# Two pairs of score tiles at a time on TensorE: one burst of products, then a projection piece behind each of the next two scores

## The chip, the cores and the metric

The kernel runs on one core of one Trainium2 chip. The metric is the time of the whole program on the device in microseconds (us), and all times here are in that unit unless another one is named. The engines are TensorE (PE, with PEld for its weight loads), VectorE (DVE), ScalarE (ACT), GpSimd (POOL) and SyncE (SP, which issues most DMAs).

## The reference

Input is x of 8 batches, 1024 tokens, 512 channels, with 16 heads of 32 channels. A block has two halves, each with a shift, a scale and a gate from a small modulation. The first half is an attention, the second a feed-forward network on the 512 tokens of each batch that a router picks. The loop of the change computes the first half:

```python
q = (x @ Wq + bq).reshape(b, h, dh, t)
k = (x @ Wk + bk).reshape(b, h, dh, t)
v = (x @ Wv + bv).reshape(b, h, dh, t)
attn = jnp.einsum('bhdt,bhds->bhts', k, v) * temperature
attn = jax.nn.softmax(attn, axis=-1)
out = jnp.einsum('bhdt,bhts->bhds', q, attn)
...
x = x + ga * _L0_attn_ref(h, ...)
```

The scores are k times v, the softmax runs over s, and the result is q times the probabilities. The reshape cuts the flat (token, channel) rows, so a head takes 64 successive tokens.

## The kernel before

The attention half runs over 8 batches of 4 groups. A group holds 4 heads (256 tokens) and 32 score tiles of 128 by 1024, called units. Two units are a pair (`p` from 0 to 15, `h2` 0 or 1), and a group has 16 pairs in two halves of 8. Seven batches run in a loop on every engine (`Fori`), the last one is written out behind it, and each engine has its own instruction stream in a fixed order; semaphores join them.

For each unit TensorE makes the score tile with two matmuls of 512 columns (`scores_of`, L551 to L560) in one of three slots of PSUM (`slot`, L361). VectorE takes the negated row maximum (`row_max`, L971 to L976). ScalarE takes the exponential with that as its bias, and sums the rows (`exp_unit`, L809 to L817); it then frees the slot (`slot_free`) for the unit three further on. The probabilities lie in eight buffers, that is four pairs. For every second pair VectorE divides q by the row sums (`q_over_sums`, L1026 to L1039, two instructions: `rinv` and `qn`). TensorE multiplies `qn` with the probabilities (`products`, L598 to L607: eight instructions of 32 output rows each), four pairs behind the scores (`LAG`), into the bank `acc`; eight pairs are summed there. VectorE then evacuates `acc` with the gate (`gated`, L1008 to L1013, after the first maximum of pairs 3 and 11), and that frees the bank for the first products of pairs 4 and 12 (`acc_free`, L680).

Beside that, TensorE computes k, v and q of the next group in sixteen pieces into one PSUM bank `pj`: four slices of k and v with three pieces of four matmuls each (`kv_slice`, L562 to L571), two slices of q with two pieces of twelve half-wide matmuls each (`q_slice`, L573 to L584). ScalarE evacuates them (`evac_kv`, after the first exponential of pairs 2, 5, 8 and 11, L850; `evac_q`, after that of pairs 13 and 15), and GpSimd adds the bias and splits them in two halves of float16 (`split_kv`, L1289 to L1298). SyncE copies the halves into the stacks that the scores of the next group read (`replicate`, L427 to L434). After pair 9 TensorE also transposes the normalised x of the group after the next into a score slot (`transposes`, L586 to L592, called at L714 to L717), and ScalarE evacuates that in four instructions (`evac_t`).

TensorE's order in a pair is: first score, the products of four pairs earlier, second score, one piece of a projection (L673 to L713). In the very last group there are no projections; there four transposes of kept tokens stand behind pairs 6, 9, 12 and 14 (L684 to L691).

VectorE's other work of a group sits between the maxima, in the order of L1104 to L1131: `qn` behind the second maximum of each even pair, the gating behind the first maximum of pairs 3 and 11, the dot product with the router behind pairs 1 and 15, statistics of x2 (the residual sum) behind pairs 5 and 7 and of the next x behind pairs 9 and 13. In the last batch it also ranks the scores of the first batch (`rank_first`, L1074).

GpSimd's work of a group hangs on `qn`: `behind_qn(b, g, j)` (L1353 to L1356) waits for the division behind pair 2j. Behind 2 it adds the residual (x2), behind 6 it splits the transposed x and multiplies h with the gate row for `base` (`base_times`, L1343), and behind 7 it adds x2 to `base` (`base_plus`, L1348), after which SyncE stores the rows (`store_rows`, L506).

Of the kernel before, what the change touches and what calls it, by code (L numbers as in the profile page):

```python
# [16 lines left out]
PAIRS = SUBS * (T // P)  # L17
GB = T // TG
NG = B * GB
# [107 lines left out]
def block_phases(nc, x, w_qkv, b_qkv, temperature, w_router, w_ffn, c, w_mod, out, h_rows, mod_rows, sel_rows, score_rows, r):  # L127
# [16 lines left out]
    with ExitStack() as ctx:  # L144
# [94 lines left out]
        aux = [pj[:], acc[:]]  # L239
# [14 lines left out]
        ft_lo = sem("ft_lo")  # L254
# [50 lines left out]
        s_ht = sem("s_ht")  # L305
# [35 lines left out]
        T_AT = 20  # L341
# [203 lines left out]
        def stk_count(b, g):  # L545

            return b * (128 * GB // 2) + 128 * (g // 2 + 1)

        @block.tensor
        def _(pe):  # L550
            def scores_of(b, g, p, h2):  # L551

                v = ring_at(p, h2)
                hq, i = 2 * (p // NQ) + h2, p % NQ
                pe.wait_ge(slot_free, freed(b, g, v))
                for half in range(2):
                    mm = nc.tensor.matmul(slot(g, v)[:, half * D:(half + 1) * D],  # L557
                                          stacks[g % 2][:, 0, hq, i * P:(i + 1) * P],
                                          stacks[g % 2][:, 1, hq, half * D:(half + 1) * D], start=True, stop=True)
                mm.then_inc(score_pe, 1)  # L560

            def kv_slice(par, kk):  # L562

                w, p = (wk16, wv16)[kk // 2], kk % 2
                terms = [(cc, a, z) for cc in range(CC) for a, z in ((0, 0), (1, 0), (0, 1))]
                for t, (cc, a, z) in enumerate(terms):
                    mm = nc.tensor.matmul(pj[:], hT16[par][:, a, cc, p * P:(p + 1) * P], w[:, z, cc, :],  # L567
                                          start=(t == 0), stop=(t == len(terms) - 1))
                    if t in (3, 7):
                        yield  # L570
                mm.then_inc(kv_pe, 1)  # L571
# [22 lines left out]
            def whole(piece):  # L594
                for _ in piece:
                    pass

            def products(p):  # L598

                i = p % NQ  # L600
                for h2 in range(2):
                    for half in range(2):
                        at = DH * (2 * h2 + half)
                        mm = nc.tensor.matmul(acc[at:at + DH, :], qn[:, (p // 2) % 2, p % 2, h2, :],  # L604
                                              probs[:, (2 * p + h2) % PROBS, half * D:(half + 1) * D],
                                              start=(i == 0), stop=(i == NQ - 1))
                return mm  # L607
# [51 lines left out]
            def transpose_kept(n, cc, dst):  # L659

                if cc == 0:
                    pe.wait_ge(s_gh[n % 2], 16 * KT * (n // 2 + 1))
                for kt in range(KT):
                    mm = nc.tensor.transpose(dst[:, kt * P:(kt + 1) * P], hs[n % 2][:, kt, cc * P:(cc + 1) * P], ident[:])
                mm.then_inc(ft_pe, 1)

            def body(b, last):
                for g in range(GB):
                    n4 = b * (GB * 4) + 4 * (g + 1)
                    n2 = b * (GB * 2) + 2 * (g + 1)  # L670
                    nxt = (g + 1) % 2
                    end = last and g == GB - 1
                    for p in range(PAIRS):  # L673
                        if p % NQ == 0:
                            for k in range(2):
                                pe.wait_ge(s_stk[k][g % 2][p // NQ], stk_count(b, g))

                        scores_of(b, g, p, 0)
                        pe.wait_ge(qn_done, b * (GB * PAIRS // 2) + g * (PAIRS // 2) + p // 2 + 1)
                        if p in (LAG, LAG + NQ):  # L680
                            pe.wait_ge(acc_free, b * (GB * SUBS) + g * SUBS + (p - LAG) // NQ + 2)
                        products((p - LAG) % PAIRS).then_inc(pv_done, 1)
                        scores_of(b, g, p, 1)
                        if end:  # L684
                            if p in KEPT_AT:
                                cc = KEPT_AT.index(p)
                                if cc == 0:
                                    pe.wait_ge(q_evac, 2 * NG)
                                else:
                                    pe.wait_ge(ft_lo, cc)  # L690
                                transpose_kept(0, cc, aux[0])  # L691
                        elif p < 12:
                            if p % 3 == 0:
                                if p == 0:
                                    pe.wait_ge(s_ht, b * GB + g + 2)
                                    pe.wait_ge(q_evac, n2)
                                else:
                                    pe.wait_ge(kv_evac, n4 + p // 3)
                                piece = kv_slice(nxt, p // 3)
                                next(piece)  # L700
                            elif p % 3 == 1:
                                next(piece)
                            else:
                                whole(piece)
                        elif p % 2 == 0:
                            if p == 12:
                                pe.wait_ge(kv_evac, n4 + 4)
                            else:
                                pe.wait_ge(q_evac, n2 + 1)
                            piece = q_slice(nxt, (p - 12) // 2)  # L710
                            next(piece)
                        else:
                            whole(piece)  # L713
                        if 2 * p + 2 == T_AT and not (last and g >= GB - 2):  # L714
                            pe.wait_ge(s_xhat, b * GB + g + 3)
                            pe.wait_ge(slot_free, freed(b, g, T_AT))
                            transposes(slot(g, T_AT))  # L717
# [522 lines left out]
        def _(pool):  # L1240
# [102 lines left out]
            def base_times(b, g):  # L1343

                par = (g + 1) % 2
                times_row(base[:, par], hbuf[:, par], 3, ALU.mult, b * (3 * GB) + 3 * g + 3)
# [6 lines left out]
            def behind_qn(b, g, j):  # L1353


                wait_alone(qn_done, b * (GB * PAIRS // 2) + g * (PAIRS // 2) + j + 2)  # L1356
# [16 lines left out]
            def body(b, last):  # L1373
                for g in range(GB):
                    n4 = b * (GB * 4) + 4 * (g + 1)
                    n3 = b * GB + g + 3
                    nxt = (g + 1) % GB
                    prep = not (last and g >= GB - 2)
                    end = last and g == GB - 1

                    behind_qn(b, g, 0)
                    if prep:
                        pool.wait_ge(t_pe, b * GB + g + 2)
                        normed_x((g + 2) % 4, n3)
                    behind_qn(b, g, 1)
                    if end:
                        gather_h(0, h_rows[0:T])
                    else:
                        split_kv(nxt, 0, n4 + 1)
                    behind_qn(b, g, 2)  # L1390
                    residual(b, g)
                    behind_qn(b, g, 3)
                    if not end:
                        split_kv(nxt, 1, n4 + 2)
                    normed_before(b, g)
                    if last and g == GB - 2:
                        wait_alone(r.s_slot, 1)
                        store_kept(nc, r, sel_rows, range(0, TB // 4))
                    behind_qn(b, g, 4)
                    if not end:  # L1400
                        split_kv(nxt, 2, n4 + 3)
                    h_times(b, g)
                    behind_qn(b, g, 5)
                    h_plus(b, g)
                    if not end:
                        split_kv(nxt, 3, n4 + 4)
                    behind_qn(b, g, 6)
                    if prep:
                        split_hT(g % 2, n3, (slot_free, freed(b, g, T_AT) + SLOTS))
                    base_times(b, g)  # L1410
                    if last and g == GB - 2:
                        store_kept(nc, r, sel_rows, range(TB // 4, TB // 2))
                    behind_qn(b, g, 7)
                    base_plus(b, g)
                    if last and g == GB - 2:
                        store_kept(nc, r, sel_rows, range(TB // 2, TB))
# [69 lines left out]
```

## Time and profile before

| | us |
|---|---|
| three runs, median (lowest to highest) | 2372.16 (2371.15 to 2373.54) |
| the profiled execution, its own time | 2367.9 |
| its span, from the first to the last instruction | 2366.2 |
| PE busy in the span | 2271.7 (96%) |
| DVE busy in the span | 1918.0 (81%) |
| ACT busy in the span | 1484.9 (63%) |
| POOL busy in the span | 1240.9 (52%) |
| granted TensorE clock, mean | 0.991 of full speed |

The attention half fills the first two thirds of the span and the feed-forward half the rest. Busy times count an instruction from its start to its end, and successive instructions of an engine overlap a little, so the distance from one start to the next is what an instruction costs a busy engine. In a timeline row the columns are the start, the duration, the engine, line and operation, the names and shapes, the number of merged instructions, and in brackets the idle time before the first and what ended it.

### The profile page before, as it was taken

The page shows a single profiled execution, that of the slowest core. Times are in us where ns is not written, and L with a number is a line of the kernel's source. Part 1 is how long each engine was busy: PE and PEld are TensorE (multiplying, and loading weights), DVE is VectorE, ACT ScalarE, POOL GpSimd, SP SyncE. Part 2 cuts the span into 40 slices and gives each one's busy share as a digit, 9 for nine tenths or more (in the row PEclk, how much of TensorE's full clock was granted, in tenths as well). Part 3 has the DMA queues.
Part 4 walks back from the last instruction along what each step waited for, and adds up shares of the span by engine and source line. Part 5 has one row for each costly group of instructions (what it writes and reads, how often), then busy time and mean ns, then how long its engine had stood idle before and what let it go on. Part 6 is the DMA issues. An engine that isn't in the chain of part 4 may idle for free.

```text
span 2366.2 us, 40899 instructions
## 1 busy us (share of the span) xinstructions
PE 2271.7 (96%) x12772; PEld 879.5 (37%) x12772; DVE 1918.0 (81%) x2908; ACT 1484.9 (63%) x2616; POOL 1240.9 (52%) x1117
## 2 busy tenths in 40 slices
PE   7999999999999999999999999887979999999998
PEld 2333333333333333333333333231434444444443
DVE  5899999999999999999999999998844654654543
ACT  1788888888888888888888888777411111111111
POOL 4666676667766667666766676554523212212300
PEclk9999999999999999999999999998989999999999
DMA  7232333333333333323334333224422021111100
GB/s 218 69 95 72 82 87 84 81 86 80 73 92 82 76 84 88 88 70 92 75 80 101 73 74 83 67 55 116 134 67 68 18 67 50 39 47 50 58 19 18
DMA packets 123765, 180.76 MB, mean 76 GB/s; under 512 B 44112, under 2 KB 44112, under 8 KB 123480
## 3 DMA queue, kind: packets, MB, share of 16 engines
q1 hardware_dynamic: 113760, 152.30, 25.9%
q0 software_dynamic: 9728, 25.23, 3.5%
q8 instruction: 117, 1.92, 0.3%
q14 instruction: 160, 1.31, 0.2%
HBM read 67.17 MB, written 43.16 MB: 47 GB/s over the span
## 4 chain that ended last, share of the span: by engine, by line
PE 57%; DVE 21%; issue 10%; POOL 5%; ACT 3%; DMA 1%; SPq 1%; DVEq 0%; POOLq 0%; ACTq 0%
DVE nmax L975 15%; PE sc L738 13%; PE sc L751 13%; PE sc L557 10%; PE acc L604 10%; PE pj L579 6%; PE pj L567 4%; POOL x L1318 3%; ACT probs L815 2%; DVE stats L1018 1%; DVE qn L1036 1%; DVE x L1013 1%; ACT room L788 1%; DVE rinv L1031 1%; POOL sel_rows L123 1%
## 5 line engine op out<-in xcount | busy, mean ns | idle before, releaser
L815 ACT ACTIVATE probs<-sc,nmax 128x1024 f32<-128x1024 f32 x1024 | 1136.7, 1116 | 240.4 <-DVE nmax L975 235.4
L975 DVE TENSOR_REDUCE nmax<-sc 128x1 f32<-128x1024 f32 x1024 | 1217.7, 1213 | 56.3 <-PE sc L557 50.0
L604 PE MATMUL acc<-probs,qn 128*32 128x512 f32 x4136 | 552.7, 607 | 9.3 <-DVE x L1013 6.7
L567 PE MATMUL pj<-room 128*128 128x512 f16 x1536 | 393.1, 379 | 0.4 <-ACT qT L805 0.4
L893 ACT ACTIVATE probs<-sc,b_col 128x512 f32<-128x512 f32 x128 | 88.0, 687 | 469.6 <-PE sc L738 440.3
L751 PE MATMUL sc<-room,probs 128*128 128x512 f16 x1536 | 352.1, 379 | 0.0
L557 PE MATMUL sc<-stacks 128*128 128x512 f16 x1024 | 309.4, 384 | 20.1 <-ACT probs L815 18.2
L557 PE MATMUL sc<-room 128*128 128x512 f16 x1024 | 307.7, 382 | 19.2 <-ACT probs L815 7.3
L1197 DVE CAST probs<-probs 128x512 f16<-128x512 f32 x128 | 58.1, 454 | 255.1 <-ACT probs L893 209.7
L751 PEld LDWEIGHTS sc<-room,probs 128*128 128x128 f16 x1536 | 150.3, 98 | 181.3
L567 PEld LDWEIGHTS pj<-room 128*128 128x128 f16 x1536 | 147.6, 98 | 187.9 <-ACT room L788 11.3
L815 ACT ACTIVATION_READ_ACCUMULATOR probs<-sc,nmax 128x1 f32 x1024 | 205.9, 201 | 0.0
L579 PE MATMUL pj<-room 128*128 128x256 f16 x1536 | 188.3, 273 | 1.1 <-ACT qT L805 0.9
L1294 POOL TENSOR_TENSOR room<-room,k_bias 128x512 f32<-128x512 f32 x64 | 81.4, 1272 | 197.7 <-DVE qn L1036 115.9
L557 PEld LDWEIGHTS sc<-stacks 128*128 128x128 f16 x1024 | 75.5, 98 | 291.3 <-ACT probs L815 185.4
L557 PEld LDWEIGHTS sc<-room 128*128 128x128 f16 x1024 | 75.7, 97 | 287.6 <-ACT probs L815 165.5
L738 PE MATMUL sc<-stacks,room 128*128 128x512 f16 x768 | 176.2, 379 | 0.0
L604 PEld LDWEIGHTS acc<-probs,qn 128*32 128x32 f32 x4136 | 81.9, 108 | 230.6 <-issue 227.0
L579 PEld LDWEIGHTS pj<-room 128*128 128x128 f16 x1536 | 150.0, 98 | 45.8 <-ACT qT L805 2.3
L1327 POOL TENSOR_TENSOR hbuf<-hbuf,rows 128x1024 f32<-128x1024 f32 x66 | 155.5, 2356 | 17.0 <-DVE qn L1036 16.7
L738 PE MATMUL sc<-qT,room 128*128 128x512 f16 x512 | 163.3, 381 | 0.1
L1298 POOL TENSOR_TENSOR room<-room 128x512 f16<-128x512 f32 x128 | 148.9, 1163 | 10.7
(146 smaller groups left out, 2241.1 us busy)
## 6 DMA issues: line engine op xcount, KB each, us to landing
room<-room SPq DMA_DIRECT2D x512, 64.0 KB, 2.0
stacks<-room SPq DMA_DIRECT2D x512, 64.0 KB, 2.0
h_rows<-hbuf SPq DMA_DIRECT2D x132, 128.0 KB, 2.3
out<-base SPq DMA_DIRECT2D x132, 128.0 KB, 2.4
room<-in_L_attn_x SPq DMA_DIRECT2D x96, 128.0 KB, 2.6
rows<-mod_rows SPq DMA_DIRECT2D x32, 256.0 KB, 3.8
room<-in_L_ffn_W SPq DMA_DIRECT2D x8, 1024.0 KB, 5.1
probs<-in_L_wmod SPq DMA_DIRECT2D x4, 1024.0 KB, 7.8
```

The lines of the kernel that those rows point to most:

```text
L557: mm = nc.tensor.matmul(slot(g, v)[:, half * D:(half + 1) * D], stacks[g % 2][:, 0, hq, i * P:(i + 1) * P], stacks[g % 2][:, 1, hq, half * ...
L567: mm = nc.tensor.matmul(pj[:], hT16[par][:, a, cc, p * P:(p + 1) * P], w[:, z, cc, :], start=(t == 0), stop=(t == len(terms) - 1))
L579: mm = nc.tensor.matmul(pj[:, ci * 2 * P:(ci + 1) * 2 * P], wq16[:, z, cc, co * P:(co + 1) * P], hT16[par][:, a, cc, :], start=(t == 0), s ...
L604: mm = nc.tensor.matmul(acc[at:at + DH, :], qn[:, (p // 2) % 2, p % 2, h2, :], probs[:, (2 * p + h2) % PROBS, half * D:(half + 1) * D], st ...
L738: mm = nc.tensor.matmul(ff[f % 2], w1_16[:, z, cc, f * P:(f + 1) * P], fT16[n % 2][a][:, cc, :], start=(t == 0), stop=(t == len(terms) - 1))
L751: mm = nc.tensor.matmul(ff2[kt], g16[:, nth(n, FC, f) % 3, a, kt * P:(kt + 1) * P], w2_16[:, z, f, :], start=(f == 0 and t == 0), stop=(f ...
L815: nc.scalar.activation(probs[:, u % PROBS, :], slot(g, ring_at(p, h2)), ACT.Exp, bias=nmax[:, u % PROBS:u % PROBS + 1], accum_out=rsum[:, ...
L893: nc.scalar.activation(g32[:, f % 2, :], ff[f % 2], ACT.Gelu_apprx_tanh, bias=b1_col[:, f:f + 1], scale=1.0 / WS).then_inc(gelu_done, 1)
L975: nc.vector.tensor_reduce(nmax[:, u % PROBS:u % PROBS + 1], slot(g, ring_at(p, h2)), AX.X, ALU.max, negate=True).then_inc(max_done, 1)
L1294: nc.gpsimd.tensor_tensor(kv32[kk % 2][:], kv32[kk % 2][:], row, ALU.add).then_inc(kv_bias, 1)
L1298: nc.gpsimd.tensor_tensor(dst[:, 1], kv32[kk % 2][:], dst[:, 0], ALU.subtract).then_inc(kv_split, 1)
L1327: nc.gpsimd.tensor_tensor(dst, a, rows[:, row:row + 1, :].broadcast_to([P, SUBS, D]), op).then_inc(s_hm, 1)
```

## The change

TensorE's loop goes in steps of two pairs. A step is: first score of the even pair, the products of both earlier pairs in one burst, second score of the even pair, a piece, first score of the odd pair, a piece, second score of the odd pair. In the steps of pairs 2 and 8 the last two are exchanged. The pieces come from one generator for the whole group, with the same waits and in the same order; the transposes stand behind the step of pair 8. On GpSimd `base_times` moves from the end of the work behind the sixth `qn` to behind the seventh.

```diff
+            def projections(b, g):
...
+                for kk in range(4):
+                    if kk == 0:
+                        pe.wait_ge(s_ht, b * GB + g + 2)
+                        pe.wait_ge(q_evac, n2)
+                    else:
+                        pe.wait_ge(kv_evac, n4 + kk)
+                    yield from kv_slice(nxt, kk)
+                    yield
+                for s in range(2):
+                    if s == 0:
+                        pe.wait_ge(kv_evac, n4 + 4)
+                    else:
+                        pe.wait_ge(q_evac, n2 + 1)
+                    yield from q_slice(nxt, s)
+                    yield
+            def first_transposes():
+                for p in range(PAIRS):
+                    if p in KEPT_AT:
...
+                        transpose_kept(0, cc, aux[0])
+                    yield
...
-                    for p in range(PAIRS):
+                    pieces = first_transposes() if last and g == GB - 1 else projections(b, g)
+                    for p in range(0, PAIRS, 2):
...
                         scores_of(b, g, p, 0)
                         pe.wait_ge(qn_done, b * (GB * PAIRS // 2) + g * (PAIRS // 2) + p // 2 + 1)
                         if p in (LAG, LAG + NQ):
                             pe.wait_ge(acc_free, b * (GB * SUBS) + g * SUBS + (p - LAG) // NQ + 2)
                         products((p - LAG) % PAIRS).then_inc(pv_done, 1)
+                        products((p + 1 - LAG) % PAIRS).then_inc(pv_done, 1)
                         scores_of(b, g, p, 1)
...
+                        next(pieces)
+                        scores_of(b, g, p + 1, 0)
+                        if p in (2, 8):
+                            scores_of(b, g, p + 1, 1)
+                            next(pieces)
                         else:
-                            whole(piece)
-                        if 2 * p + 2 == T_AT and not (last and g >= GB - 2):
+                            next(pieces)
+                            scores_of(b, g, p + 1, 1)
+                        if 2 * p + 4 == T_AT and not (last and g >= GB - 2):
                             pe.wait_ge(s_xhat, b * GB + g + 3)
                             pe.wait_ge(slot_free, freed(b, g, T_AT))
                             transposes(slot(g, T_AT))
...
                     if prep:
                         split_hT(g % 2, n3, (slot_free, freed(b, g, T_AT) + SLOTS))
-                    base_times(b, g)
                     if last and g == GB - 2:
                         store_kept(nc, r, sel_rows, range(TB // 4, TB // 2))
                     behind_qn(b, g, 7)
+                    base_times(b, g)
                     base_plus(b, g)
```

## Rows read from the trace of the kernel before

**Rows 1.** The page, chain that ended last: shares of the span by engine.
```profile
PE 57%; DVE 21%; issue 10%; POOL 5%; ACT 3%; DMA 1%; SPq 1%; DVEq 0%; POOLq 0%; ACTq 0%
```

**Rows 2.** Timeline of TensorE, group 1 of batch 4: scores, products, pieces.
```profile
899.06 0.59 PE L557 MATMUL sc<-stacks 128*128 128x512 f16 x2
...
904.71 0.59 PE L557 MATMUL sc<-stacks 128*128 128x512 f16 x2
905.24 1.07 PE L604 MATMUL acc<-probs,qn 128*32 128x512 f32 x8
906.24 0.60 PE L557 MATMUL sc<-stacks 128*128 128x512 f16 x2
906.68 1.03 PE L567 MATMUL pj<-room 128*128 128x512 f16 x4
907.54 0.59 PE L557 MATMUL sc<-stacks 128*128 128x512 f16 x2
...
936.44 1.47 PE L579 MATMUL pj<-room 128*128 128x256 f16 x12
...
947.58 0.59 PE L557 MATMUL sc<-room 128*128 128x512 f16 x2
```

**Rows 3.** Timeline of all engines around the transposes of that group.
```profile
926.32 1.11 ACT L815 ACTIVATE probs<-sc,nmax 128x1024 f32<-128x1024 f32 x1
...
927.58 1.09 PE L590 MATMUL sc<-ident,room 128*128 128x128 f32 x8
...
928.72 0.61 PE L557 MATMUL sc<-stacks 128*128 128x512 f16 x2
...
929.37 1.23 DVE L975 TENSOR_REDUCE nmax<-sc 128x1 f32<-128x1024 f32 x1 [0.28 <-PE sc L557]
```

**Rows 4.** Timeline of all engines, that group: VectorE's rows of k0 to k3.
```profile
905.19 0.85 DVE L1004 SCALAR_TENSOR_TENSOR dot_out<-hbuf,router_row 128x512 bf16<-128x512 f32 x1
...
905.98 2.34 DVE L975 TENSOR_REDUCE nmax<-sc 128x1 f32<-128x1024 f32 x2
...
908.24 0.16 DVE L1031 RECIPROCAL rinv<-rsum 128x4 f32<-128x4 f32 x1
...
908.65 1.22 DVE L975 TENSOR_REDUCE nmax<-sc 128x1 f32<-128x1024 f32 x1
...
909.78 0.68 DVE L1013 TENSOR_TENSOR x<-acc,rows 128x512 f32<-128x512 f32 x1
...
910.38 3.47 DVE L975 TENSOR_REDUCE nmax<-sc 128x1 f32<-128x1024 f32 x3
...
913.77 0.17 DVE L1031 RECIPROCAL rinv<-rsum 128x4 f32<-128x4 f32 x1
...
916.90 0.69 DVE L1018 BATCH_NORM_STATS2 stats<-x 128x6 f32<-128x512 f32 x1 [0.31 <-POOL x L1318]
...
922.44 0.68 DVE L1018 BATCH_NORM_STATS2 stats<-x 128x6 f32<-128x512 f32 x1
...
923.43 2.32 DVE L975 TENSOR_REDUCE nmax<-sc 128x1 f32<-128x1024 f32 x2
```

**Rows 5.** Timeline of all engines, that group: ScalarE's rows of k1.
```profile
907.30 1.11 ACT L815 ACTIVATE probs<-sc,nmax 128x1024 f32<-128x1024 f32 x1 [0.79 <-DVE nmax L975]
...
908.41 0.68 ACT L788 ACTIVATE room<-pj,tempw_col 128x512 f32<-128x512 f32 x1
...
908.98 1.11 ACT L815 ACTIVATE probs<-sc,nmax 128x1024 f32<-128x1024 f32 x1
...
911.63 1.11 ACT L815 ACTIVATE probs<-sc,nmax 128x1024 f32<-128x1024 f32 x1 [0.35 <-DVE nmax L975]
```

**Rows 6.** Timeline of TensorE at the end of attention: products of two pairs.
```profile
1658.57 1.92 PE L604 MATMUL acc<-probs,qn 128*32 128x512 f32 x16
```

**Rows 7.** Timelines of GpSimd and of SyncE's queue at that group's end.
```profile
945.37 2.37 POOL L1351 TENSOR_TENSOR base<-base,x 128x1024 f32<-128x1024 f32 x1 [0.33 <-DVE qn L1036]
...
938.99 10.02 SPq L433 DMA_DIRECT2D room<-room  x16
```

## What I predict, and from what

> **What bounds the kernel now.** I read the page's chain first [rows 1]: TensorE holds 57% of it and VectorE 21%, so in the attention loop two engines take turns. Then I read the timeline of one steady group (group 1 of batch 4) engine by engine; a "cycle" is two pairs, four score tiles a, b, c, d, and k0 to k7 are the eight cycles of a group.
>
> TensorE [rows 2]: from a pair's first score to its products 0.53, products to second score 1.00, second score to the piece 0.44, piece 0.86. That is 2.83 a pair, 5.66 a cycle. A piece of q products is 1.47 long against 1.03, so it takes 0.45 more: 1.31, and such a cycle (k6, k7) 6.55. The transposes of k4 take 1.14 [rows 3]. Six times 5.66, twice 6.55 and 1.14 are 48.20; the group took 48.52 (899.06 to 947.58) [rows 2]. So TensorE waited 0.32 in a whole group, and it looks like the bound.
>
> VectorE [rows 4]: two maxima take 2.26 (905.98 to 908.24), so one takes **1.13**; reciprocal and qn 0.41; the gating between c and d 0.60 (909.78 to 910.38); the dot of k0 0.79; the statistics about 0.61, with the aggregate of k3 0.99. From 905.98 to 923.43, three cycles, it paused only for x2 (0.31 before 916.90): 5.82 a cycle, more than TensorE's 5.66. TensorE's first scores stood at 904.71 and, three cycles later, at 921.69; VectorE took them up 1.27 and 1.74 later. **VectorE already sets the pace in k1 to k4**, and the three score slots let TensorE hide it until the transposes.
>
> The ring [rows 3, 5]: a score tile's maximum can start 0.65 after its first matmul (928.72 to 929.37), its exponential 1.25 after the maximum began (910.38 to 911.63; I use 1.26), and the score that takes over the slot 1.26 after the exponential began (926.32 to 927.58). So a slot turns round in at least 3.17, plus whatever VectorE or ScalarE is late.
>
> **The change part by part.**
>
> *The burst.* Products of two pairs follow each other. At the end of attention the trace has such a burst, 16 matmuls of 1.92 [rows 6], 0.85 more than the 1.07 of eight [rows 2]; 1.00 + 0.85, rounded up to 1.86, against twice 1.00. One switch from score to products becomes score to piece, 0.44 for 0.53. A cycle of TensorE is then 0.53 + 1.86 + 0.44 + 0.86 + 0.44 + 0.86 + 0.44 = **5.43** (before 5.66), with q pieces **6.33** (before 6.55). Unheld, a group is 6 x 5.43 + 2 x 6.33 + 1.14 = 46.38, which is 1.82 under 48.20. In k1 and k4 the order c, d, piece has the same sum. The Trainium skill ("TensorE: Matmul & The Clock Gate", Part 3) says that a weight load overlaps running matmuls only where the row groups differ; products use all 128 rows, so by it the second pair would cost its full 1.00 and the burst 2.00. The row at the end of attention gives 1.86; the other value is a rival below.
>
> *The slot of b.* The next a uses the slot of b. Before, b started 1.53 behind a, and the next a 4.13 behind b. Now b starts 2.39 behind a, and the next a is due 3.04 behind b, less than the 3.17 of an idle ring. So even with every other engine ready a cycle is 5.56, and each tenth by which VectorE or ScalarE is late holds TensorE up. VectorE is late: that is the step on which I decide.
>
> *The walk.* I carry the three engines through a group by the rows above, times from its first score, with VectorE 2.00 behind at a. F is when b's slot is free (its maximum plus 2.52, or later where ScalarE is held); "due" is TensorE unheld.
>
> | k | a | max a | max b | F | due | next a | held |
> |---|---|---|---|---|---|---|---|
> | 0 | 0 | 2.00 | 3.13 | 5.65 | 5.43 | 5.65 | 0.22 |
> | 1 | 5.65 | 7.72 | 8.85 | 11.90 | 11.08 | 11.90 | 0.82 |
> | 2 | 11.90 | 13.25 | 14.93 | 17.45 | 17.33 | 17.45 | 0.12 |
> | 3 | 17.45 | 19.80 | 20.93 | 23.45 | 22.88 | 23.45 | 0.57 |
> | 4 | 23.45 | 25.72 | 26.85 | 29.90 | 28.88 | 31.04 | 1.02 |
> | 5 | 31.04 | 31.69 | 34.07 | 36.59 | 36.47 | 36.59 | 0.12 |
> | 6 | 36.59 | 38.56 | 40.06 | 42.58 | 42.92 | 43.36 | 0.44 |
> | 7 | 43.36 | 45.29 | 46.42 | 48.94 | 49.69 | 49.69 | 0 |
>
> Line k1 in full. VectorE ends k0 at 2.00 + 4 x 1.13 + 0.41 + 0.79 = 7.72 and does a, then b at 8.85. ScalarE starts a's exponential at 8.98, needs 1.11 for it (907.30 to 908.41) and then, before b's, does the evacuation of a projection, 0.57 (908.41 to 908.98) [rows 5]: 8.98 + 1.11 + 0.57 + 1.26 = 11.92, in the table 11.90. TensorE was due at 5.65 + 5.43 = 11.08. In the other lines: k2, b is ready only at 14.29 + 0.65, so VectorE idles 0.55, and the statistics wait for x2 as now (3.13 behind the reciprocal at 913.77) [rows 4]; k4, the same evacuation, and the transposes take b's slot, so the 1.02 falls before them; k5, VectorE has caught up at a and waits 1.25 for b behind the burst; k6, the burst waits for the gating (begins at 36.83, 0.68 long, plus 0.05) where it was due at 37.12. That wait is old, but the products now stand 2.27 behind the start of c instead of 3.36; behind it are queued the burst, b, c and d, and VectorE's b. k7 ends with VectorE 1.94 behind, so the walk closes on itself.
>
> The holds add up to 3.31 and the gain was 1.82: a group of **49.69 against 48.52, 1.17 more**. VectorE's account agrees: from b of k0 to b of k4 it needs 23.72, before 4 x 5.82 or some 23.3; the gains of the q cycles are less than what it idles at b of k2, k5 and k6.
>
> *What costs nothing.* The odd pair's products move ahead of a score and a piece; they need the same qn as the even pair's, so no wait is new there, and the exponential of a waits for products that end 1.6 behind a's start, before its maximum ends. The kept-token transposes keep their piece numbers. GpSimd's multiplication for base moves behind the next qn: with the addition (2.37, ending 0.16 into the next group now) [rows 7] it ends some 3 into the next group, before GpSimd's next call at the qn of k0 (4.7). SyncE's stores then wait for it; now they wait until 949.01, 1.43 into the group, for the copies of the stacks, so they come up to 2 later, and SyncE has nothing else urgent until x2 of k2. Were that cover gone, the price would be those 2 once a group, 56 in all; the other end is a gain of the little that it hinders qn of k7, under 0.4, in a cycle where VectorE is not what ends last. I take 0. The second stack copies start behind the last projection split; eight of the sixteen (half of 10.02) [rows 7] are needed by the next group, and the walk leaves them about half a microsecond.
>
> **The sum.** 28 groups in the seven looped batches by 1.17 are 33. The last batch's first three groups have ranking work on VectorE; between 0 and 1.17 each, I take 0.5 each, 1.5 in all, because a longer VectorE cycle gives the slots more time. The last group has no projections: 0. Together +34 on the profiled execution's 2367.9, which gives 2402. The median of the runs is 4.3 above that execution, so **2406**. About 0.2% is what a measurement of this kernel can tell from no change.
>
> **Rivals.**
> 1. *The slots only just hold* (faster). If VectorE is never behind at b, a cycle is 5.56 and a group 6 x 5.56 + 2 x 6.33 + 1.14 with the old 0.32 of waits, 47.48: 1.04 x 28 or 29 less, **2343**. For it: TensorE's near-full timeline, with little waiting. Against it: the growing lag of 1.27 to 1.74. It decides at b: where VectorE takes b up at once and no evacuation lies between, F meets the due time to about a tenth.
> 2. *VectorE keeps its pace everywhere*: it is late but never idles at b of k2, k5 and k6, so only the q cycles gain, 0.14 and 0.25 a group: 11 less, **2361**. Against it: a's lead is used up at the transposes.
> 3. *Holds and gains cancel*, with the lag a few tenths smaller: **2372**.
> 4. *The burst is no cheaper than its parts*, 2.00, the change not doing what it says: 0.14 a cycle, passed on in about five cycles of eight, 0.7 x 28 or 20 more than forecast: **2426**. Against it stands the burst of rows 6, so its chance is small.
>
> **How the numbers follow.** Forecast 0.67 (its own range 2390 to 2425: holds 0.4 a group either way, and the last batch), rival 1 0.08, rival 2 0.12, no change 0.07, rival 4 0.06. Faster 0.20, same 0.07, slower 0.73. The range 2355 to 2428 takes in the forecast, rivals 2, 3 and 4, and leaves rival 1 out.
>
> **What would show it.** Right: bursts of 16 at 1.86; groups of 49.7; TensorE idle some 3.3 a group before a, named for the exponentials, most in k1 and k4; VectorE idle over a microsecond for b in k5. Wrong: groups of 47.5 with hardly a wait at a (rival 1), or VectorE without pauses (rival 2); then the walk's lag at a is the step that failed.

## The result, and the profile after

| | before | after |
|---|---|---|
| median of four runs each (lowest to highest) | 2372.60 (2371.15 to 2373.54) | 2474.57 (2470.43 to 2476.25) |
| span of the profiled execution | 2366.2 | 2474.5 |

The ratio is 1.0428, 95% interval 1.041 to 1.0446: the changed kernel is 102 us slower. The forecast was 2406 with a range up to 2428, so the sign was right and the size was not.

The page of after: busy time of the engines, shares of the chain that ended last [rows 1], and two of the costliest groups (count | busy, mean ns of one | idle before them, and what ended most of it).

```profile
PE 2273.3 (92%) x12772; PEld 909.4 (37%) x12772; DVE 1956.1 (79%) x2908; ACT 1490.1 (60%) x2616; POOL 1243.8 (50%) x1117
...
PE 52%; DVE 23%; issue 13%; ACT 5%; POOL 4%; DMA 1%; SPq 1%; DVEq 1%; ACTq 0%; POOLq 0%
...
L986 DVE TENSOR_REDUCE nmax<-sc 128x1 f32<-128x1024 f32 x1024 | 1215.5, 1214 | 121.1 <-PE sc L557 116.3
L604 PE MATMUL acc<-probs,qn 128*32 128x512 f32 x4136 | 516.8, 619 | 25.9 <-DVE x L1024 21.3
```

TensorE is as busy as before (2271.7), in a longer span. Two lines say where to look. VectorE's maxima sat idle for 121.1 waiting for scores (56.3 before), which the walk foresaw. And VectorE's busy time grew from 1918.0 to 1956.1, by 38, though it has the same 2908 instructions: something on it became longer, and the prediction has no step for that.

TensorE's timeline of one group of after (start, duration, form, and in brackets the idle time before), from the first score behind the loop's jump to the first score of the next group:

```profile
901.72 0.60 PE L557 MATMUL sc<-room 128*128 128x512 f16 x2 [2.00 <-issue]
...
913.44 0.61 PE L557 MATMUL sc<-room 128*128 128x512 f16 x2
...
925.04 0.60 PE L557 MATMUL sc<-room 128*128 128x512 f16 x2 [0.46 <-ACT probs L826]
...
932.58 0.61 PE L557 MATMUL sc<-room 128*128 128x512 f16 x2
933.11 1.92 PE L604 MATMUL acc<-probs,qn 128*32 128x512 f32 x16
934.97 0.60 PE L557 MATMUL sc<-room 128*128 128x512 f16 x2
...
939.03 1.92 PE L604 MATMUL acc<-probs,qn 128*32 128x512 f32 x16 [0.30 <-DVE x L1024]
...
951.31 0.60 PE L557 MATMUL sc<-stacks 128*128 128x512 f16 x2
```

These are a of k0, k2, k4 and k5 and of the next k0. From the first they stand at 0, 11.72, 23.32, 30.86 and 49.59; the walk has 0, 11.90, 23.45, 31.04 and 49.69. The burst is 1.86 (933.11 to 934.97), and k6's burst waits for the gating. This group is the walk. The next one is not: it takes 51.48 (to 1002.79), and nearly all of the excess over the walk (1.69 of 1.79) is in its k0, which takes 7.34 where the walk has 5.65. The timeline of all engines of after at that place:

```profile
949.68 2.35 POOL L1338 TENSOR_TENSOR base<-hbuf,rows 128x1024 f32<-128x1024 f32 x1 [2.32 <-DVE qn L1047]
...
951.31 0.60 PE L557 MATMUL sc<-stacks 128*128 128x512 f16 x2
...
952.11 2.37 POOL L1362 TENSOR_TENSOR base<-base,x 128x1024 f32<-128x1024 f32 x1
...
952.47 2.57 DVE L1015 SCALAR_TENSOR_TENSOR dot_out<-hbuf,router_row 128x512 bf16<-128x512 f32 x1
...
954.97 2.34 DVE L986 TENSOR_REDUCE nmax<-sc 128x1 f32<-128x1024 f32 x2
...
957.56 0.60 PE L557 MATMUL sc<-stacks 128*128 128x512 f16 x2 [1.09 <-ACT probs L826]
...
958.65 0.61 PE L557 MATMUL sc<-stacks 128*128 128x512 f16 x2 [0.49 <-ACT probs L826]
```

Before, `base_plus` ended 0.16 into the group [rows 7]; VectorE's timeline of before, which the prediction does not show at that place, has the router dot of pair 15 beginning 0.13 ahead of that end:

```profile
947.61 0.68 DVE L1004 SCALAR_TENSOR_TENSOR dot_out<-hbuf,router_row 128x512 bf16<-128x512 f32 x1
```

Now `base_times` stands in front of it, `base_plus` runs from 952.11 to 954.48, and the dot, which reads `hbuf` and `router_row` beside it, takes 2.57 and ends 0.56 after it. The two maxima behind it start at 954.97, 3.66 behind a (the walk has 2.00), and TensorE then waits 1.09 and 0.49 for slots. Over the whole run the dots by their line (shortest, median and longest in ns; the median was 682 before):

```profile
L1015 DVE SCALAR_TENSOR_TENSOR dot_out<-hbuf,router_row x67: 674/1005/2882, 76.2 to 1827.2; 128x512 bf16<-128x512 f32 x67
```

Theory from here: the burst costs what the walk says, about +34, and the move of `base_times` the rest, because a VectorE instruction with two operands in SBUF stands still while GpSimd works on SBUF. The rival: the burst costs it all and the long dot lies in slack.

### The profile page after: what moved, and what is told of

Read it like the earlier page. It is cut to its first block, busy times and chain, and to the rows that moved or that the text cites. A ratio compares the mean times of both kernels' runs of the same rounds, so it can differ in the third digit from the quotient of the medians.

```text
span 2474.5 us, 40899 instructions
## 1 busy us (share of the span) xinstructions
PE 2273.3 (92%) x12772; PEld 909.4 (37%) x12772; DVE 1956.1 (79%) x2908; ACT 1490.1 (60%) x2616; POOL 1243.8 (50%) x1117
## 3 DMA queue, kind: packets, MB, share of 16 engines
q8 instruction: 117, 1.92, 0.3%
## 4 chain that ended last, share of the span: by engine, by line
PE 52%; DVE 23%; issue 13%; ACT 5%; POOL 4%; DMA 1%; SPq 1%; DVEq 1%; ACTq 0%; POOLq 0%
DVE nmax L986 14%; PE sc L749 12%; PE sc L762 12%; PE acc L604 11%; PE sc L557 7%; PE pj L579 6%; ACT probs L826 3%; POOL x L1329 3%; DVE dot_out L1015 3%; ACT room L799 1%; DVE x L1024 1%; PE pj L567 1%; DVE stats L1029 1%; DVE qn L1047 1%; DVE rinv L1042 1%
## 5 line engine op out<-in xcount | busy, mean ns | idle before, releaser
L986 DVE TENSOR_REDUCE nmax<-sc 128x1 f32<-128x1024 f32 x1024 | 1215.5, 1214 | 121.1 <-PE sc L557 116.3
L604 PE MATMUL acc<-probs,qn 128*32 128x512 f32 x4136 | 516.8, 619 | 25.9 <-DVE x L1024 21.3
L557 PE MATMUL sc<-stacks 128*128 128x512 f16 x1024 | 304.3, 384 | 68.9 <-ACT probs L826 67.2
L604 PEld LDWEIGHTS acc<-probs,qn 128*32 128x32 f32 x4136 | 111.2, 111 | 303.3 <-issue 275.1
```

Of the source, the lines that this page charges most:

```text
L986: nc.vector.tensor_reduce(nmax[:, u % PROBS:u % PROBS + 1], slot(g, ring_at(p, h2)), AX.X, ALU.max, negate=True).then_inc(max_done, 1)
```

## The experiments

**1. The burst alone.** After, with `base_times` back in its old place.

```diff
                     behind_qn(b, g, 6)
...
+                    base_times(b, g)
...
                     behind_qn(b, g, 7)
-                    base_times(b, g)
```

> The changed kernel with GpSimd's base_times put back behind the sixth qn; the bursts stay. Theory A (the move costs the missing part): base_plus no longer runs beside the router dot of pair 15, which is 0.68 again instead of 2.57; VectorE is about 2 behind at a of k0 instead of 3.7, and a group takes 49.7 to 50.0 as the walk of the prediction said. Time 2405 to 2425. Rival B (the burst alone accounts for it, and the long dot only fills time that VectorE has to wait anyway): 2465 to 2475, the groups as long as in the changed kernel.

Measured: 2420.27 (2418.99 to 2423.25), ratio 1.0209 [1.0193, 1.0224]. By the distances between the transposes, groups within a batch take 49.79 (before mostly 48.52, the walk 49.69), and the dot is back at a median of 683 ns. Two successive rows of transposes from TensorE's timeline, and the dots by their line:

```profile
908.47 1.10 PE L590 MATMUL sc<-ident,room 128*128 128x128 f32 x8
...
958.25 1.09 PE L590 MATMUL sc<-ident,room 128*128 128x128 f32 x8
```

```profile
L1015 DVE SCALAR_TENSOR_TENSOR dot_out<-hbuf,router_row x67: 673/683/2828, 76.5 to 1776.2; 128x512 bf16<-128x512 f32 x67
```

So the burst costs +50, and the change's other 54 are the move: the theory's place is right.

**2. The move alone.** Before, with `base_times` behind the seventh `qn`.

```diff
-                    base_times(b, g)
...
                     behind_qn(b, g, 7)
+                    base_times(b, g)
```

> The kernel before with only base_times moved behind the seventh qn, no bursts. Theory A: base_times and base_plus run without a pause over the router dot of pair 15, which comes close to the end of base_times. If the dot is held until base_plus ends it takes 2.5 to 3.1 instead of 0.68, VectorE enters k0 some 2 later and never catches up before the transposes: 1.2 to 1.6 a group more, 2405 to 2425. If the dot gets in between the two it takes about 0.9 and the time is 2372 to 2380. Rival B: 2372, no change, whatever the dot takes.

Measured: 2399.34 (2395.38 to 2401.91), ratio 1.0126 [1.011, 1.0141]: between the two theories' numbers. Two of three groups within a batch grow to 50.22 and 50.54, the third stays at 48.56. The timeline of all engines of this kernel in a long and a short one:

```profile
913.64 2.37 POOL L1351 TENSOR_TENSOR base<-base,x 128x1024 f32<-128x1024 f32 x1
...
913.81 2.75 DVE L1004 SCALAR_TENSOR_TENSOR dot_out<-hbuf,router_row 128x512 bf16<-128x512 f32 x1
...
964.04 0.68 DVE L1004 SCALAR_TENSOR_TENSOR dot_out<-hbuf,router_row 128x512 bf16<-128x512 f32 x1
964.17 2.78 POOL L1351 TENSOR_TENSOR base<-base,x 128x1024 f32<-128x1024 f32 x1
```

Where the addition starts first (by 0.17), the dot takes 2.75; where the dot starts first (by 0.13), it takes its 0.68 and the addition 2.78 instead of 2.37. Whoever comes second waits. Which it is hangs on a tenth of a microsecond, and that is why the price is paid in two groups of three. The group across the loop's jump has the long dot too and pays nothing: 49.87 to 50.21, before 49.57 to 50.32. With the bursts every looped group has the long dot, and every group within a batch pays. So the two parts of the change don't add up: 50 and 29 alone, 102 together.

The Trainium skill ("SBUF — State Buffer", section "Who interferes with whom") says that a VectorE instruction with two inputs in SBUF contends with a GpSimd instruction that reads SBUF, for ports that are an exclusive lock, and that "Issue order, not op shape, decides who blocks." Both rows agree, the short dot as well as the long one.

**3. Take away only the overlap.** After, with one wait on GpSimd: `base_plus` starts behind the dot of pair 15.

```diff
                     base_times(b, g)
+                    wait_alone(s_dot, b * (2*GB) + 2*g + 2)
                     base_plus(b, g)
```

> The changed kernel as it is, bursts and move, but base_plus waits for the router dot of pair 15. Nothing else differs, so this is the contention by itself. Theory A: the dot is 0.68 to 0.9, a group 49.6 to 50.0, time 2405 to 2425, like the burst alone; base_plus ends a microsecond later and nobody waits for it. Rival B: 2470 or more, since GpSimd's work only gets later.

Measured: 2425.23 (2419.83 to 2426.85), ratio 1.0224 [1.0207, 1.0241]; the interval overlaps that of experiment 1. Groups of 49.79 again, and the timeline of all engines:

```profile
925.56 2.36 POOL L1338 TENSOR_TENSOR base<-hbuf,rows 128x1024 f32<-128x1024 f32 x1 [2.30 <-DVE qn L1047]
...
928.34 0.68 DVE L1015 SCALAR_TENSOR_TENSOR dot_out<-hbuf,router_row 128x512 bf16<-128x512 f32 x1
...
929.20 2.36 POOL L1362 TENSOR_TENSOR base<-base,x 128x1024 f32<-128x1024 f32 x1 [1.28 <-DVE dot_out L1015]
```

`base_times` is still late, and `base_plus` and the stores behind it are later than in after, yet the 49 us are gone (2474.57 to 2425.23). So it is neither the late stores nor GpSimd's own work; it is the overlap with the dot.

**4. The burst only where a cycle is long.** Before, with the step of two pairs only for p of 12 and 14, where a cycle is 6.33 and the slot of b has time.

```diff
+if p < 12:
+    for q in (p, p + 1):
...
+else:
+    scores_of(b, g, p, 0)
...
+    products((p - LAG) % PAIRS).then_inc(pv_done, 1)
+    products((p + 1 - LAG) % PAIRS).then_inc(pv_done, 1)
+    scores_of(b, g, p, 1)
+    next(pieces)
+    scores_of(b, g, p + 1, 0)
+    next(pieces)
+    scores_of(b, g, p + 1, 1)
```

> Bursts only in the last two cycles of a group (pairs 12 to 15, with the long q pieces), the old order in the other six, base_times at its old place. By the walk (theory A) the slot of b has 3.9 there, so nothing is held and 0.22 is saved twice a group, 0.44 x 28 to 31 or 12 to 14 us: 2358 to 2361. If VectorE sets the pace in these cycles too: 2372, no change. Rival B (a burst costs more than the turn-round of its slot): slower than 2372.

Measured: 2386.80 (2385.01 to 2386.99), ratio 1.0066 [1.0052, 1.008]; groups of 48.95. VectorE's timeline at the end of a group:

```profile
899.50 1.23 DVE L992 TENSOR_REDUCE nmax<-sc 128x1 f32<-128x1024 f32 x1 [0.89 <-PE sc L557]
...
902.99 1.23 DVE L992 TENSOR_REDUCE nmax<-sc 128x1 f32<-128x1024 f32 x1 [0.52 <-PE sc L557]
...
909.29 1.22 DVE L992 TENSOR_REDUCE nmax<-sc 128x1 f32<-128x1024 f32 x1 [0.52 <-PE sc L557]
910.43 0.68 DVE L1021 SCALAR_TENSOR_TENSOR dot_out<-hbuf,router_row 128x512 bf16<-128x512 f32 x1
```

VectorE waits 0.89 for b behind the burst and 0.52 for each fourth score behind its piece: 1.93 in the two cycles. It leaves the group late and pays in the next one, where it sets the pace. The expected 2358 to 2361 counted only TensorE's gain.

**5. The same, with both scores ahead of the burst.** Order for p of 12 and 14: a, b, burst, c, piece, d, piece; TensorE does the same work as in experiment 4.

```diff
 scores_of(b, g, p, 0)
+scores_of(b, g, p, 1)
...
 products((p + 1 - LAG) % PAIRS).then_inc(pv_done, 1)
-scores_of(b, g, p, 1)
-next(pieces)
 scores_of(b, g, p + 1, 0)
 next(pieces)
 scores_of(b, g, p + 1, 1)
+next(pieces)
```

> As the run with bursts only in the last two cycles, but both scores of the even pair stand ahead of the burst and each piece behind a score of the odd pair: a, b, burst, c, piece, d, piece. TensorE's work is the same. Theory A (what counts is when VectorE gets its tiles): b comes 1.95 earlier, the last piece covers d's maximum and the dot, and VectorE enters the next group 0.65 behind as in the kernel before, not 1.95; a group is 48.1 against 48.5, time 2356 to 2362 where the kernel before has 2371. Rival B (a burst costs there whatever the order): 2383 to 2390, as the run with the scores around the burst.

Measured: 2376.78 in ten runs (2372.92 to 2382.99), ratio 1.0027 [1.0017, 1.0038], between the times of theory A and rival B. Groups within a batch take 48.37 to 48.46, shorter than before (48.51 to 48.84) by 4.1 in the 21 of the run: with VectorE served first the burst gains a little, 0.2 a group where 0.4 was expected. The six groups across the loop's jump give back 6.1 and the first group 1.6. Two of those six took 52.47 and 52.50, the others 50.06 to 50.39. Stretches around one of the long ones (start and end, length, busy time of PE, PEld, DVE, ACT, POOL, granted clock, share and GB/s of the DMA):

```profile
650.00:655.00 5.00, 4.98 (x38) 2.48 (x39) 4.96 (x9) 4.00 (x9) 4.67 (x3) 1.00 0.47 107
655.00:658.00 3.00, 1.07 (x10) 0.71 (x8) 1.71 (x3) 3.00 (x6) 1.15 (x1) 1.00 0.29 67
658.00:663.00 5.00, 4.56 (x17) 1.09 (x18) 2.02 (x2) 1.25 (x3) 0.00 (x0) 0.66 0.64 140
663.00:668.00 5.00, 5.00 (x31) 1.42 (x29) 4.91 (x9) 3.62 (x6) 3.06 (x5) 1.00 0.48 126
```

TensorE was busy for 1.07 of three microseconds, and in the next five the granted clock was 0.66 of full, so the engine ran part of them at the lower of its levels (1.2 against 2.4 GHz).

**6. The order of experiment 5 from pair 10 on.**

```diff
-if p < 12:
+if p < 10:
```

> The same order, in the last three cycles (pairs 10 to 15). By the walk, the cycle behind the transposes takes 5.97 in this order against 5.76 in the old one, because b waits for the slot of d and the burst stands in front of c: 48.3 a group, 2362 to 2370. If the burst's saving of 0.23 came through there too: 2350 to 2356. Rival B: above 2385.

Measured: 2381.27 (2377.57 to 2384.43), ratio 1.0045 [1.0031, 1.006]; groups of 48.81, a miss of all three expected times: one more short cycle costs 0.4 a group against experiment 5, where the walk had 0.2 and the other case a gain.

**7. The order of experiment 5 in all cycles.** In the steps of pairs 2 and 8 the first piece goes ahead of c.

```diff
 scores_of(b, g, p, 0)
+scores_of(b, g, p, 1)
...
+if p in (2, 8):
+    next(pieces)
+    scores_of(b, g, p + 1, 0)
+else:
+    scores_of(b, g, p + 1, 0)
+    next(pieces)
+scores_of(b, g, p + 1, 1)
+next(pieces)
```

> The burst in all eight cycles in the order a, b, burst, c, piece, d, piece (a piece ahead of c in the steps of pairs 2 and 8), base_times at its old place. TensorE's instructions and their number are those of the run with the burst alone. Theory A: VectorE has two tiles to work on during the burst and idles at none of k2, k5, k6; the slot of c is now the tight one (free 5.19 plus VectorE's lag behind a, due 5.87). The walk gives 48.3 a group, and some 0.3 more in each of the two cycles with the early piece: 48.6 to 49.0, time 2372 to 2390. Rival B (the burst itself costs): 49.8 a group and 2415 to 2425.

Measured: 2410.91 (2407.52 to 2413.81), ratio 1.0176 [1.0161, 1.019]; groups of 49.70 and 49.97, outside both expected times and nearer to the rival. TensorE's timeline:

```profile
922.38 1.03 PE L557 MATMUL sc<-stacks 128*128 128x512 f16 x4
...
925.20 0.60 PE L557 MATMUL sc<-stacks 128*128 128x512 f16 x2
925.64 1.03 PE L567 MATMUL pj<-room 128*128 128x512 f16 x4
926.50 0.59 PE L557 MATMUL sc<-stacks 128*128 128x512 f16 x2
...
927.80 1.25 PE L557 MATMUL sc<-stacks 128*128 128x512 f16 x4
...
933.74 0.61 PE L557 MATMUL sc<-stacks 128*128 128x512 f16 x2
934.93 0.61 PE L557 MATMUL sc<-stacks 128*128 128x512 f16 x2 [0.58 <-ACT probs L826]
```

The rows of scores are a with b, c, d, then the next a with b. Now b is the one held: it takes the slot of c. Unheld it would start 0.44 behind a, as the piece does behind c (925.20 to 925.64), and so (927.80 + 0.44) − 925.20 = 3.04 behind c, again under the 3.17 of the ring. The pair of scores takes 1.25 instead of 1.03 there, and 0.58 is lost where a later slot waits for its exponential. Two orders, two slots, one result.

**8. What stands last before the loop's jump.** Experiment 1, with the order c, d, piece in the step of pair 14 too. This was to explain why the groups across the jump are dearer than the walk.

```diff
-                        if p in (2, 8):
+                        if p in (2, 8, 14):
```

> The first experiment's kernel with one more exchange: in the step of pair 14 too the fourth score goes ahead of the second piece, so that a q piece (1.47 long) and no score (0.59) stands last before the jump of the loop. Theory A: what TensorE still has queued at the jump covers a part of the pause behind it; then the pause at the loop's end is 0.7 to 0.9 shorter than the 2.37 to 2.61 of the first experiment, as in the kernel before and the seventh (1.7, 1.6), stretches at half clock behind it become rarer, the six groups across the jump are 50.2 to 52 instead of a mean of 52.6, and the groups within a batch 49.3 to 49.8, since VectorE's wait of 0.5 for the fourth tile of k7 goes: 2400 to 2413 in all. Theory B: the pause has its own length whatever stands ahead of it; it stays at 2.4 or more, the groups across the jump stay near 52.6 and the time within 2412 to 2423.

Measured: 2420.20 (2418.78 to 2424.23), ratio 1.0211 [1.0194, 1.0228]: the time of experiment 1, so theory A falls. The pause at the jump stays at 2.31 to 2.80; TensorE's timeline at one of the six:

```profile
870.72 1.47 PE L579 MATMUL pj<-room 128*128 128x256 f16 x12
875.00 0.60 PE L557 MATMUL sc<-room 128*128 128x512 f16 x2 [2.80 <-issue]
```

No run shows what sets the length of that pause. The DMA records of before and of experiments 1 and 8 have one thing in common at all 18 of their jumps: a 16 KB transfer of an instruction queue (q8) begins 2.7 to 3.5 ahead of the first score behind the jump and ends 1.7 to 2.0 ahead of it; elsewhere in the loop such transfers come some 10 to 20 apart. So the loading of instructions is the likeliest cause, argued and not tried.

No version was faster than before; the nearest is experiment 5.

## Why the prediction was wrong, step by step

- **What costs nothing: failed, and cost most.** "I take 0" for the move of `base_times` asked who waits for GpSimd (its own next call, SyncE's stores). It even named a VectorE instruction that the old place hinders, the qn of k7, but it did not ask which one stands beside the new place. The rows were there: the addition ended 0.16 into the group [rows 7] and the dot of pair 15 begins 0.03 into it; `base_times` in front, 2.4 long, puts one on the other. Timelines of before also show the size: that qn takes 0.66 beside `base_times` where most take 0.29, and in the last batch, where the addition comes first, the dot takes 2.08.

```profile
942.69 2.35 POOL L1327 TENSOR_TENSOR base<-hbuf,rows 128x1024 f32<-128x1024 f32 x1
...
944.54 0.66 DVE L1036 TENSOR_TENSOR qn<-qT,rinv 128x128 f32<-128x128 f32 x1
...
1601.33 2.40 POOL L1351 TENSOR_TENSOR base<-base,x 128x1024 f32<-128x1024 f32 x1
...
1602.20 2.08 DVE L1004 SCALAR_TENSOR_TENSOR dot_out<-hbuf,router_row 128x512 bf16<-128x512 f32 x1
```

The term put at 0 measured 54 (experiment 1) or 49 (experiment 3). That the bound of 56 lies near is luck: it stood for late stores, which experiment 3 rules out.

- **The burst: right.** 1.92 long in mid-stream as in rows 6, and 1.86 to the next score; rival 4, with 2.00, did not come.
- **The slot of b and the walk: right.** The groups within a batch of experiment 1 are on average 1.19 longer than before (24.9 in 21), forecast 1.17. From a to a its cycles k0 to k7 take 5.64, 6.46, 5.56, 6.05, 7.55, 5.55, 6.68 and 6.31; the walk has 5.65, 6.25, 5.55, 6.00, 7.59, 5.55, 6.77 and 6.33. VectorE idles 1.17 for b in k5 (walk 1.25) and 0.55 in k2, as in the walk. From start to start the holds of such a group are 49.78 − 46.38 = 3.40, where the prediction's sign of being right has some 3.3 of idle time; as idle time its rows show only 1.76, since successive instructions overlap. TensorE had 1.82 a group to gain and lost more to the three slots.
- **The sum: too small at the edges.** Experiment 1 is the forecast's own case, +50 by the medians where I had +34. Its profiled span is 55.3 over before's, and the transposes split that: within a batch 24.9 (forecast 24.6), across the jump 15.9 for six groups (7.0), the first group 4.1 (1.2), the last batch 9.8 (1.5), the rest 0.6. I had priced every group alike, though the groups at the jump, in the last batch and at the start have pauses of another kind. At the jump TensorE pauses for 0.97 to 1.73 in before and for 1.83 to 2.61 in experiment 1, and stretches at the lower clock follow three of those six. In the last batch the burst of both pairs waits for one gating, and its products then run at the lower clock, as TensorE's timeline of experiment 1 shows:

```profile
1522.95 3.09 PE L604 MATMUL acc<-probs,qn 128*32 128x512 f32 x16 [3.06 <-DVE x L1024]
...
1583.92 2.62 PE L604 MATMUL acc<-probs,qn 128*32 128x512 f32 x16 [3.06 <-DVE x L1024]
...
1643.08 3.57 PE L604 MATMUL acc<-probs,qn 128*32 128x512 f32 x16 [2.48 <-DVE x L1024]
```

The kernel before waits 1.98 and 1.99 at the first two of these places and not at the third, so only the rest of the waits is new. That these waits and the slower bursts behind them carry the last batch's 9.8 is argued from the rows; no run took them away.

- **The rivals.** 1 and 2 needed a VectorE that keeps up, and the walk had said why it does not. None had a dearer VectorE instruction in it.

## What to carry to other kernels

When a GpSimd instruction moves, lay its new place against VectorE's timeline, not only against what waits for it: a VectorE instruction with two operands in SBUF there is paid until GpSimd's ends (the dot, and the qn of before), while a maximum read from PSUM next to it is not: in before the 53 maxima that lie wholly beside `base_times` or `base_plus` take 1.21 to 1.23, all others 1.16 to 1.23. Where another engine sets the pace through a ring of buffers, a cheaper sequence on the fuller engine gives nothing unless each slot's distance from its fill to its reuse stays above the ring's turn-round; write that distance down for every slot of the new order. Holding it is not enough where the new order feeds the slower engine later (experiment 4). Price the groups at a loop's jump and at the ends by rows of their own.

## What the runs showed of the hardware that was not expected

- The dot and GpSimd's addition exclude each other as wholes: 0.68 becomes 2.54 to 2.88 in the 28 looped groups of after, and a head start of 0.13 turns it round (experiment 2).
- TensorE's clock falls behind some pauses and not behind others. In the looped batches of before no burst of products runs at half clock. In after seven of them do (2.87 to 3.62 for 16 matmuls where 1.92 is usual), in experiment 1 four, in experiment 8 one. The stretch of after around one of them, with a pause of 1.59, and the next:

```profile
589.00:594.00 5.00, 2.92 (x14) 0.91 (x11) 4.96 (x8) 2.34 (x5) 1.25 (x4) 1.00 0.61 137
594.00:599.00 5.00, 5.00 (x25) 1.22 (x24) 3.73 (x5) 3.47 (x6) 2.33 (x3) 0.66 0.54 91
```

In the five microseconds ahead TensorE was busy for 2.92; then 0.66 was granted. The same place of a later batch (799 to 804, TensorE again busy for 2.92, the same pause of 1.58 against 1.59) is followed by five microseconds at 1.00, and behind the pauses of up to 2.80 of experiment 8 the bursts take their 1.92. So idle time of TensorE can cost more than its own length, and when it does could not be told from these runs. Five of the 21 groups within a batch of after hold such a burst; they take 52.85 to 53.15, the other sixteen 51.64 to 51.97, so by an estimate (five times the difference of their means, 1.2) some 6 of the move's 54 come by way of the clock. Falls of the clock are also the likeliest cause, not a shown one, of the spread of experiment 5: its four fastest executions have a mean granted clock of 0.987, its three slowest 0.984 or 0.985.
